# Two expert layers: places of their own for the outputs of single blocks, and their rows loaded ahead

## The reference, cut to what matters

```python
# layer 0: one expert for each token
top1 = argmax(x @ gate_W + gate_b)
out  = sum over e of (gelu(x @ W1[e] + b1[e]) @ W2[e] + b2[e]) where top1 == e
# layer 1: two experts for each token, weighed by the gates, limited by a capacity
ye   = gelu(xe @ W1 + b1) @ W2 + b2
out  = ye[idx1, pos1] * w1 * keep1 + ye[idx2, pos2] * w2 * keep2
```

## Time and profile before

| | us |
|---|---|
| median of 3 runs | 1060.05 |
| the runs | 1060.01, 1060.05, 1069.24 |
| the profiled execution's own time | 1055.93 |
| its span, first to last instruction | 1054.1 |
| blocks of the first expert layer in it | about 319 to 407 |
| blocks of the second | about 878 to 1025 |

### The profile page before, as it was taken

How to read it: one execution, slowest core, us unless ns; L and a number is a source line. 1 busy time by engine, 2 the same in 40 slices (tenths; PEclk the granted TensorE clock), 3 DMA queues, 4 the chain that set the end, 5 groups by cost and what they waited for, 6 DMA issues and landing times.

```text
span 1054.1 us, 21432 instructions
## 1 busy us (share of the span) xinstructions
PE 965.7 (92%) x6330; PEld 695.2 (66%) x6330; DVE 691.8 (66%) x2589; ACT 631.3 (60%) x1945; POOL 650.7 (62%) x803
## 2 busy tenths in 40 slices
PE   5788799999998978999999999999898899999965
PEld 2565466666668976666665665556666788999955
DVE  6977777886773324867778677677885574445634
ACT  4348767767765546677776775766665564444432
POOL 4663588788756543676686668788746651555540
PEclk9789999999999999999999999999999999999997
DMA  9400202302337764033031230321222035787758
GB/s 292 78 7 1 47 27 62 73 26 60 84 104 181 216 204 117 6 75 65 16 70 25 46 70 26 70 56 50 55 66 68 31 102 136 227 231 226 214 168 240
DMA packets 95444, 103.20 MB, mean 98 GB/s; under 512 B 10095, under 2 KB 83030, under 8 KB 95088
## 3 DMA queue, kind: packets, MB, share of 16 engines
q1 hardware_dynamic: 88752, 89.36, 33.4%
q0 software_dynamic: 6592, 12.65, 3.5%
HBM read 77.54 MB, written 23.50 MB: 96 GB/s over the span
## 4 chain that ended last, share of the span: by engine, by line
PE 54%; DVE 18%; ACT 8%; POOL 7%; issue 6%; DMA 5%; SPq 1%; POOLq 0%; DVEq 0%; ACTq 0%
PE bank L1285 10%; PE bank L772 7%; PE bank L1314 7%; PE bank L783 7%; PE bank L1341 5%; DVE arena L1973 5%; ACT arena L1697 4%; PE bank L1329 4%; PE bank L1304 4%; PE bank L1364 3%; DMA expert_out<-RA 2%; DVE arena L1982 2%; DMA expert_out<-arena 2%; POOL arena L1071 2%; DVE arena L1873 2%
## 5 line engine op out<-in xcount | busy, mean ns | idle before, releaser
L1697 ACT ACTIVATE arena<-arena 128x128 f32<-128x128 f32 (+1 forms) x512 | 226.9, 446 | 102.1 <-DVE arena L1973 101.8
L1973 DVE CUSTOM_DVE_ANT_0 arena<-bank,arena 128x128 f32<-128x128 f32 (+1 forms) x512 | 183.1, 413 | 115.2 <-PE bank L1314 112.3
L1285 PE MATMUL bank<-arena 128*128 128x512 f32 x384 | 211.4, 637 | 7.7 <-ACT arena L1686 5.2
L1071 POOL TENSOR_TENSOR arena<-arena 128x512 f32<-128x512 f32 x128 | 133.3, 1045 | 127.8 <-ACT arena L1673 108.7
L1982 DVE COPY arena<-bank 128x384 f32<-128x384 f32 x256 | 130.1, 549 | 21.3 <-PE bank L1329 21.0
L1086 POOL TENSOR_TENSOR arena<-arena 128x512 f32<-128x512 f32 x128 | 129.8, 1050 | 1.3
L1673 ACT ACTIVATE arena<-bank 128x512 f32<-128x512 f32 x192 | 112.7, 587 | 27.7 <-PE bank L1285 27.4
L1329 PEld LDWEIGHTS bank<-const,arena 128*128 128x128 f32 x768 | 91.4, 142 | 55.6 <-issue 55.2
L738 POOL DMA_INDIRECT expert_out<-arena x71 | 71.3, 1005 | 90.8 <-DVE arena L868 40.5
L1314 PE MATMUL bank<-arena 64*128 64x128 f32 (+1 forms) x1024 | 118.5, 350 | 6.6 <-DVE arena L1973 6.0
L1341 PE MATMUL bank<-arena 128*64 128x256 f32 (+1 forms) x1024 | 112.2, 340 | 6.6 <-DVE arena L1982 6.2
(11 more groups left out here) (302 smaller groups left out, 1641.3 us busy)
## 6 DMA issues: line engine op xcount, KB each, us to landing
arena<-in_wp SPq DMA_DIRECT2D x40, 514.0 KB
arena<-recip_rows SPq DMA_DIRECT2D x30, 512.0 KB, 6.4
XN<-in_wp SPq DMA_DIRECT2D x24, 514.0 KB
arena<-expert_rows SPq DMA_DIRECT2D x46, 129.0 KB
arena<-in_b SPq DMA_DIRECT2D x64, 64.0 KB
arena<-expert_out SPq DMA_DIRECT2D x16, 256.0 KB, 5.2
expert_out<-fill SPq DMA_DIRECT2D x11, 338.6 KB
expert_rows<-fill SPq DMA_DIRECT2D x1, 2644.5 KB, 21.7
```

Of the source, the lines that this page charges most:

```text
L1071: pool.tensor_tensor(sq[:, i % 2], r, r, ALU.mult).then_inc(S["sq_done"], 1)
L1285: mm = pe.matmul(RING[bnk][:, :], xa[:, p, t * P:(t + 1) * P], wqkv[:, 512 * k:512 * k + 512], start=True, stop=True)
L1697: ins = act.activation(w, w, ACT.Exp, bias=nm[:, p, 16 * t + h:16 * t + h + 1], scale=-1.0, accum_out=den[:, p, 16 * t + h:16 * t + h + 1])
L1973: ins = v.tensor_tensor_reduce(out=SPb[:, c % 2, 384 * k + P * t:384 * k + P * t + n], in0=SBANK[k][:, P * t:P * t + n], in1=alibi[:, h, N ...
```

## The change

Outputs and row numbers no longer go by `j % 4` in all blocks. A table `PLACES` gives each block a place. Places 0 to 3 are the old buffers; places from 4 on are small buffers of their own (`OWN`, one row of 129 words for each partition: 128 outputs and the row number). In layer 0 there are three of them: blocks 15, 16, 17 take them, 18 to 21 go back to the four old ones in the order 3, 0, 1, 2, and 22 and 23 take the first two of their own again. In layer 1 all nine single blocks have a place of their own. All places of their own share the semaphore `sent4`. `evac_x` waits for a scatter only where the place is one of the old four, and once at block 22 of layer 0. Weights, b2, rows and the turned rows keep their four (or two) buffers.

The single blocks' rows of layer 1 have buffers of their own too (`SROWS`). SP loads five of them in the loop over double blocks, one a round, and four in its steps 20 to 23; the row loads of the single blocks in its later steps are gone. TensorE waits for all nine before it turns the first.

```diff
+NOWN = (3, NSMALL)
+PLACES = (tuple(j % 4 if j < 15 else (4, 5, 6, 3, 0, 1, 2, 4, 5)[j - 15] for j in range(NBIG[0] + NSMALL)),
+          tuple(j % 4 if j < NBIG[1] else 4 + j - NBIG[1] for j in range(NBIG[1] + NSMALL)))
+NPLACES = 4 + 1
+AGAIN = (22, None)
...
+        SROWS = take(NSMALL * ROW).rearrange("p (k d) -> p k d", k=NSMALL)
+        YROWS1 = take(NOWN[1] * ROW).rearrange("p (k d) -> p k d", d=ROW)
...
+        def outputs(layer, j, q):
+            k = place(layer, j, q)
+            n = 1 if single(layer, j, q) else 2
+            return OWN[layer][:, k - NBUF, 0:D] if k >= NBUF else FFNB[layer][5][:, k, 0:n * D]
+        def sent_by(layer, k, last):
+            return sum(16 if m in SMALL[layer] else 32 for m in range(last) if min(PLACES[layer][m], NBUF) == k)
+        def sender(layer, j, q):
+            return f"sent{min(place(layer, j, q), NBUF)}"
...
+            def load_single(k):
+                at_ = k + NBIG[1]
+                row = sp.value_load(rowtab[1][0:1, bass.ds(at_, 1)], min_val=0, max_val=NOROWS)
+                dst = SROWS[:, k] if isinstance(k, int) else SROWS[:, bass.ds(k, 1)].rearrange("p k d -> p (k d)")
+                sp.dma_start(dst, xe[1][bass.ds(row, BLK), :]).then_inc(S["single_rows"], 16)
...
                 load_weights(j + NBUF, q, i + 1)
-                if more:
+                if layer and q == 1 and not isinstance(j, int):
+                    load_single(i)
+                if layer and isinstance(j, int) and last <= j < last + NSMALL - last // NBUF:
+                    load_single(j - last + last // NBUF)
+                if more and not (layer and single(1, j + NBUF + 2 if isinstance(j, int) else j, q)):
                     sp.wait_ge(S["xT_evac"], j + (base + 3))
                     load_rows(j + NBUF + 2, (q + 2) % NBUF, i + (q + 2 + NBUF) // NBUF)
...
             def turn(j, q, i):
+                if layer and single(1, j, q):
+                    pe.wait_ge(S["single_rows"], NSMALL * 16)
+                    mm = pe.transpose(XT[q % 2][:, 0:P], SROWS[:, j - NBIG[1], 0:D], ident)
...
             def evac_x(j, q, i):
                 v.wait_ge(S["xT_full"], j + (base + 1))
-                if layer or not isinstance(j, int) or j >= NBUF:
-                    v.wait_ge(S[f"sent{q}"], sends(layer, j, q, i))
+                if place(layer, j, q) < NBUF and (layer or not isinstance(j, int) or j >= NBUF):
+                    v.wait_ge(S[sender(layer, j, q)], sends(layer, j, q, i))
+                if j == AGAIN[layer]:
+                    v.wait_ge(S[f"sent{NBUF}"], sent_by(layer, NBUF, j))
```

More of the change, by code:

```diff
@@ L665, in entry, with place, numbers @@
             return i * (NBUF - len(few)) + (len(few) + q - k)
+        def place(layer, j, q):
+            return PLACES[layer][j] if isinstance(j, int) else q
+        def outputs(layer, j, q):
+            k = place(layer, j, q)
+            n = 1 if single(layer, j, q) else 2
+            return OWN[layer][:, k - NBUF, 0:D] if k >= NBUF else FFNB[layer][5][:, k, 0:n * D]
+        def numbers(layer, j, q):
+            k = place(layer, j, q)
+            n = 1 if single(layer, j, q) else 2
+            return OWN[layer][:, k - NBUF, D:D + 1].bitcast(I32) if k >= NBUF else FFNB[layer][6][:, k, 0:n]
+        def sent_by(layer, k, last):
+            return sum(16 if m in SMALL[layer] else 32 for m in range(last) if min(PLACES[layer][m], NBUF) == k)
+        def sender(layer, j, q):
+            return f"sent{min(place(layer, j, q), NBUF)}"
         def sends(layer, j, q, i):
-            before = layer * sum(16 if m in SMALL[0] else 32 for m in range(q, NBLK0, NBUF))
+            k = place(layer, j, q)
+            before = layer * sent_by(0, k, NBLK0)
             if isinstance(j, int):
-                return before + sum(16 if m in SMALL[layer] else 32 for m in range(q, j, NBUF))
-            n = 16 if q in SMALL_OF_FOUR[layer] else 32
-            return i * n + (before + 32 - n)
+                return before + sent_by(layer, k, j)
+            return i * 32 + before
         def ffn_sync(sp, layer, nblk, base, scattered, first_rows=None):
@@ L749, in all_sent @@
         def all_sent(eng, layer):
-            for q in range(NBUF):
-                eng.wait_ge(S[f"sent{q}"], sends(layer, (NBLK0, NBLK1)[layer], q, 0))
+            for k in range(NPLACES):
+                eng.wait_ge(S[f"sent{k}"], layer * sent_by(0, k, NBLK0) + sent_by(layer, k, (NBLK0, NBLK1)[layer]))
         HBANKS = (bank[2:6], bank[4:6] + bank[2:4])
@@ L876, in silu2 @@
                 n = D if single(layer, j, q) else 2 * D
-                v.scalar_tensor_tensor(out=yb[:, q, 0:n], in0=th[:, q % 2, 0:n], scalar=1.0, in1=yb[:, q, 0:n], op0=ALU.add,
+                v.scalar_tensor_tensor(out=outputs(layer, j, q), in0=th[:, q % 2, 0:n], scalar=1.0, in1=outputs(layer, j, q), op0=ALU.add,
                                        op1=ALU.mult).then_inc(S["y_ready"], 1)
```

31 lines of the change are left out of this document (17 added, 14 removed).

## The result

Both kernels were timed 20 times each, run in turn. The changed kernel has a median of 1055.1 us (1051.02 to 1063.21), the kernel before 1061.62 us (1055.88 to 1069.24). The ratio of the changed kernel to the one before is 0.9944, with a 95% interval of 0.9924 to 0.9963: 5.9 us of 1061.6, between 4 and 8. The forecast was 10.4 us. So it went the way that was forecast, and a little more than half as far.

What follows compares the result with a forecast made beforehand. Single blocks were taken to be bound by scatter landings that delay VectorE's copies and stall TensorE; first layer -6.5, second -4.3, contention +0.4 make -10.4 us, from 1060.05 to 1049.6 us, range 1046 to 1056.

Steps and rivals of the forecast that it cites:

- What bounds the stretch, and what the change removes: Single blocks of both layers: waits for scatters of four blocks before stall TensorE 14.8 us; the new places remove them.
- What is late next: Single blocks of both layers: once scatter waits go, the 514 KB weight loads, issued after the add four blocks before.
- the recurrence over three blocks: Second layer: up to add 2.38, SP 0.74, landing 4.0, so three blocks per 7.1 us; -4.3 us.
- The price of a weight load: Single blocks' weights: 4.0 us from SP's issue to usable data, range 3.7 to 5.0.
- rival B: Single blocks: weights land near 5.0 us, each load queued behind the one before; -7.4 us, 1052.7 us; chance 28%.
- 0.4 for contention: Double blocks: nine row loads moved there take DMA time while scatters wait; 0.4 us lost, ends 0 and 2.1.
- SP as the first layer's limit: First layer's single blocks: SP still issues row loads, 2.74 us a block when behind; -6.5 us.
- Rows loaded ahead at nothing on SP: Double blocks with a moved row load: SP's step becomes 3.85 us beside TensorE's 3.73, covered by weight slack; costs nothing.
- The sum: Whole kernel: -6.5 - 4.3 + 0.4 = -10.4 us, giving 1049.6 us; chance 44% for a gain of 8.5 to 12.5.
- A: Single blocks of both layers: weights land sooner, in 3.2 us; -12.8 us, 1047.2 us; chance 17%.
- C: First layer's blocks 18 to 21 still wait for scatters; gain about 7 us or less, 1053 us; chance 4%.
- D: Single blocks of both layers: the clock falls to 1.2 GHz and stays; 11 us slower, 1071 us; chance 7%.

Runs made afterwards that it cites:

- rows_only: The changed kernel with all outputs and row numbers back in the four old buffers, layer 1's single rows still loaded ahead; 1.0013 of the kernel before.
- small_weights: The changed kernel with each single block's weight load cut to 128 of 1028 words a partition; 0.9907 of the kernel before.
- places_only: The changed kernel with layer 1's single rows loaded in SP's steps again, the new places kept; 0.9935 of the kernel before.
- before_again: The kernel before, unchanged, profiled again on another chip; median 1088.39 us.
- value_early: The changed kernel with SP reading the next expert's number before its wait for the add; 0.9874 of the kernel before.
- early_again: Second run of the changed kernel with SP's expert number read ahead of its wait; 0.9905 of the kernel before, median 1050.75 us.
- places_early: The changed kernel without layer 1's single rows loaded ahead, with SP's expert number read ahead of its wait; 0.9922 of the kernel before.

## Why the prediction was half right

- **What bounds the stretch, and what the change removes: right.** The scatters' waits went, nothing of the four old places made a single block wait, the tail and the attention behind kept their lengths, and `rows_only` shows that the gain is the places'. One thing the prediction did not count went too: the clock of 0.50 among the first layer's single blocks (389.6 to 393.0 us before, there in three of the four traces with the old places, in none of the twelve with the new).
- **What is late next: right.** TensorE's new waits are for weights, with the recurrence over three blocks as it was written.
- **The price of a weight load: wrong, and this is the step that failed.** "I take 4.0, near the lower end, since data seen to have moved is the nearer evidence." It was 4.95, the upper end within 0.05 us. The old trace was not read far too low: there the last increment came 4.2 us after the issue (median), and 4.3 to 4.4 us for the two loads that the prediction used. The failed assumption is that this price stays when the pace changes. In the new pace it was 4.84 us, and TensorE began some 0.1 us behind it. So of the 0.95 us, 0.2 were missed in the old pace, some 0.6 came with the new one, and 0.1 is from increment to use. Loads that share the DMA engines with the one before would do this, which is rival B's reason, and `small_weights` points the same way; no run isolates it.
- **What the measured price gives.** With 4.95 in the prediction's own sums, block 20's up is at 384.8 + 4.95 = 389.75, block 23's weights, which are issued once block 19 is added, land at 389.75 + 2.38 + 0.74 + 4.95 = 397.8 (-4.8 us), and the second layer's up(39) is at 1002.6 + 8.07 x 2 = 1018.7 (-2.5 us): with the 0.4 for contention 6.9 us, where 5.9 were measured. The first layer's part was 3.9 in the trace. Of the missing 0.9, 0.8 lie at its start: the weights of block 18 went out 1.57 us after block 14's add ended (382.35 to 383.92), not 0.74, because SP was behind; its issue of b2 at 380.86 took 1.17 us in place of 0.35.
- **SP as the first layer's limit: about right.** Its issues are 2.76 to 2.97 us apart where it is behind; but the landing round of 2.7 us would give the same, and with the true landing it has a share in the last two blocks.
- **Rows loaded ahead at nothing on SP, 0.4 us of contention: not shown wrong.** The steps of blocks 20 to 23 took 3.94 us, as costed at 3.85; from 955 us on TensorE stood still for no double block but the last, by 0.6 us, where it was 0.4 before. `places_only` and the change differ by less than their intervals.
- **The sum.** The forecast of 1049.6 us against the median before of three runs, 1060.05; with 20 runs that median is 1061.6 and the changed one 1055.1. Rival B, loads that land near 5.0 us, had the mechanism and gave -7.4 us, 1052.7 us, within the measured interval of 4 to 8 us. It had 28%, and its reason is the one that the increments bear out. It deserved more: the forecast named the closer pace and the DMA share of 0.84, and then priced the load as if neither mattered.
- **The other rivals.** A (landing in 3.2 us, by the estimate from the Trainium skill, "DMA: Bandwidth & Descriptors", section "Anatomy of one DMA — SWDGE (gpsimd) path") is refuted: even 64 KB needed 3.6 us until use. That fit is for DMAs that GpSimd issues, and these are SP's. By the 436 GB/s that the Trainium skill states in that section, an estimate, the 450 KB would be 1.03 us, for 1.35 measured with the neighbours' loads shrunk as well. C did not occur. D, the slower one, did not either: the clock stayed at 1.00 through both stretches of single blocks.

## What to carry to other kernels

When a wait is taken away, the next one sets the gain: write the round through it (here add, issue, landing, up, down, over three blocks) and put into it the landing until use, at the new pace, not at the old one: here it went from 4.2 to 4.9 us when the loads came closer together. Without an awaited load the last semaphore increment in the trace gives the old price. A register read behind a wait is part of that round, and to move it ahead of the wait was worth about as much as the change itself, though only after the change. An earlier transfer is good only where its destination waits for it: given to all blocks, it went with longer waits for the scatters of the first layer's double blocks.

## What the runs showed of the hardware that was not expected

At the entry of the first expert layer TensorE stands still for some 1.7 us, in two pieces (1.23 and 0.51), in all kernels. In 12 of 16 traces the granted clock then fell to 0.50, the 1.2 GHz level, for about 3 us (the window at 320 us above shows 0.57), and from the first up-projection to the next it took 3.2 to 3.7 us in place of 2.05. The four that kept 1.00 were before, before_again, rows_only and value_early; early_again, the same program as value_early, had the dip. So the same program does both, and it costs 1.1 to 1.6 us. With the old places one trace of four had it, with the new ones eleven of twelve. Whether the change makes it more frequent, and so gives back part of its gain, stays open: the expert layers' code is all that differs, and it begins only here.

With the old places the clock also fell among single blocks: in the first layer in three traces of four, in the second in two of four. The new places had it there in one of twelve (places_early, second layer).
